# A conditional gated MLP with per-sequence adapters, recut from one fused pass over tiles into two phases with the activation spilled to DRAM

## The chip, the cores and the metric

The kernel runs on one core of one Trainium2 chip. The metric is device microseconds from start to end of one execution; lower is better. The engines named below are TensorE (PE in the profile, PEld for its weight loads), VectorE (DVE), ScalarE (ACT), GpSimd (POOL, which issues the indirect DMAs) and SyncE (SP, which issues the plain DMAs).

## What is computed

`x` is 64 sequences of 32 rows of 512 numbers. Each sequence has an adapter index (`itok_B_2_6`, 16 possible) for the rank-16 additions of the MLP, and a second index (`itok_B_0_15`) for a 32x32 mixing matrix over its rows. All is float32.

```python
def lora_add(base, inp, A, B):
    Ab = A[layer_idx][lora_indices]
    Bb = B[layer_idx][lora_indices]
    t = jnp.einsum('bri,bni->bnr', Ab, inp)
    return base + jnp.einsum('bor,bnr->bno', Bb, t) * SCALE
gate = lora_add(jnp.einsum('bnh,fh->bnf', x, W_gate), x, A_gate, B_gate)
up = lora_add(jnp.einsum('bnh,fh->bnf', x, W_up), x, A_up, B_up)
act = jax.nn.silu(gate) * up
down = lora_add(jnp.einsum('bnf,hf->bnh', act, W_down), act, A_down, B_down)
...
x = x + down                                  # F = 1376, H = 512, rank 16, SCALE 0.5
x = x + jnp.einsum('bct,bcd->bdt', x, weights[itok_B_0_15])   # 32x32 per sequence
```

## The kernel before

A tile is 4 sequences, 128 rows; there are 16 tiles, and one loop body (`tile`) does a whole tile on each engine. Every float32 product is made of three passes of a reduced-width type (fp32r): each operand is split into a high part (`hi`, a copy by ACT, L346) and a remainder (`lo`, a subtraction by DVE, L446), and PE multiplies hi*hi, hi*lo and lo*hi. The weights are loaded once through four slots of `landing`, split, and stay in SBUF for the whole run (`w_gate_hi`, `w_gate_lo`, `w_up_*`, `wd_*`).

In a tile PE computes gate and up in three sections of 352, 512 and 512 columns (`base`, L641 to L643, four blocks of 128 input features each), adds the adapters' part (`lora`, L650 and L651), transposes the gated activation through PE with an identity matrix (`turn_act`, L662, 11 chunks of 128 columns into the bank `ps_turn`), and multiplies the transposed chunks with the down weights (`down_chunks`, L673, 66 instructions of 288 columns). The down adapter (`down_lora`, L683) and the mixing (`mix`, L692) of a tile are done in the next tile, between its gate and up products, so that nothing waits for them. ACT does silu (L381) and the high parts, DVE the gating product (L528), the low parts, the masking and 32x32 turning of the adapters' small products (`mask_t`, `mask_td`), the two residual additions (`residual_h` L516, `residual_out` L523) and the spreading of the mixing matrix into a block diagonal `mix_w` (`spread_mix`, L509). POOL gathers by index: four of `a_raw` (the A factors of gate, up and down together), one of `b_raw` (all B factors, 3264 columns) and one of `mix_raw` (L322, L325, L333). SP loads `xT` and `x` and stores the result.

The order on every engine is written out by hand; engines meet only in semaphores. In `gathers(t)` POOL waits until the previous tile's `a_raw` and `b_raw` were split, gathers the next ones, and then waits for `mix_ready`, that is for `spread_mix` of the previous tile on DVE.

Of the kernel before, what the change touches and what calls it, by code (L numbers as in the profile page):

```python
# [17 lines left out]
TILES = SEQS // TILE_SEQS  # L42
KH = H // P
RR = TILE_SEQS * RANK
SECTIONS = [(0, F - 1024), (F - 1024, 512), (F - 512, 512)]
NS = len(SECTIONS)
SECTION_CHUNKS = [[(c, min(P, c0 + n - c)) for c in range(c0, c0 + n, P)] for c0, n in SECTIONS]
CHUNKS = [c for chunks in SECTION_CHUNKS for c in chunks]
FIRST_CHUNK = [sum(map(len, SECTION_CHUNKS[:s])) for s in range(NS + 1)]
SHORT = next(i for i, (_, n) in enumerate(CHUNKS) if n < P)  # L50
NC = len(CHUNKS)
TC = 2 * RR
A_GU = KH * 2 * RANK
A_ROW = A_GU + NC * RANK
B_ROW = 2 * F + H
WD = H + RR
HALF = WD // 2
HALVES = [slice(0, HALF), slice(HALF, H)]
PIECE = 1024
SLOTS = 4  # L60

def weight_pieces():

    pieces = [(m, s, k) for s in range(NS) for m in ("gate", "up") for k in range(0, KH, 2)]
    c = 0
    while c < NC:
        n = 1 if c == SHORT or c + 1 in (SHORT, NC) else 2
        pieces.append(("down", c, n))  # L70
        c += n
    return pieces

PIECES = weight_pieces()
GU_PIECES = sum(m != "down" for m, _, _ in PIECES)

def pieces_to(m, s, k):

    return PIECES.index((m, s, k - k % 2)) + 1

def pieces_to_chunk(c):
    return next(i for i, (m, at, n) in enumerate(PIECES) if m == "down" and at <= c < at + n) + 1

def build(nc, x, xT, w_gate, w_up, w_down, a_rows, b_rows, mix_rows, which, mult, lane, low, out):
    with ExitStack() as ctx:
        def sb(name, shape, dt=F32):  # L90
            return ctx.enter_context(nc.sbuf_tensor(name, shape, dt))

        def bank(name):
            return ctx.enter_context(nc.psum_tensor(name, [P, 512], F32))
# [3 lines left out]

        w_cols = {"gate": KH * (F + TC), "up": KH * F}
        w_hi = {m: sb(f"w_{m}_hi", [P, w_cols[m]], F32R) for m in ("gate", "up")}
        w_lo = {m: sb(f"w_{m}_lo", [P, w_cols[m]], F32R) for m in ("gate", "up")}
        wd_hi = sb("wd_hi", [P, NC, WD], F32R)
        wd_lo = sb("wd_lo", [P, NC, WD], F32R)
        landing = sb("landing", [P, SLOTS, PIECE])

        a_raw = sb("a_raw", [P, TILE_SEQS, A_ROW])
        b_raw = sb("b_raw", [P, B_ROW])
        b_gu = sb("b_gu", [P, 2 * F], F32R)  # L110
        b_dn = sb("b_dn", [P, H], F32R)

        xT_raw = sb("xT_raw", [P, KH * P])
        xT_hi = sb("xT_hi", [P, KH * P], F32R)
        xT_lo = sb("xT_lo", [P, KH * P], F32R)
        x_sb = sb("x_sb", [P, H])
        out_sb = sb("out_sb", [P, H])

        t_gu = sb("t_gu", [P, 2, 2 * RR])
        t_dn = sb("t_dn", [P, 2 * RR])  # L120
        tT_raw = sb("tT_raw", [P, 2, P])
        tdT_raw = sb("tdT_raw", [P, P])
        low_rows = sb("low_rows", [P, 1])
        tT_hi = sb("tT_hi", [P, 2, P], F32R)
        tT_lo = sb("tT_lo", [P, 2, P], F32R)
        tdT_hi = sb("tdT_hi", [P, P], F32R)
        tdT_lo = sb("tdT_lo", [P, P], F32R)
        act = [sb(f"act{i}", [P, 512]) for i in range(2)]
        actT_hi = sb("actT_hi", [P, NC, P], F32R)
        actT_lo = sb("actT_lo", [P, NC, P], F32R)  # L130

        mix_raw = sb("mix_raw", [P, CH])
        mix_w = sb("mix_w", [P, P])

        ident = sb("ident", [P, P])
        mask = sb("mask", [P, 2 * RR])
        which_sb = sb("which_sb", [P, TILES, TILE_SEQS + 2], I32)
        mult_sb = sb("mult_sb", [P, TILE_SEQS + 2], I32)
        lane_sb = sb("lane_sb", [P, TILE_SEQS + 2], I32)
        scaled = sb("scaled", [P, TILES, TILE_SEQS + 2], I32)  # L140
        rows = sb("rows", [P, TILES, TILE_SEQS + 2], I32)
        waited = sb("waited", [1, 1], I32)
        rows_now = sb("rows_now", [P, TILE_SEQS + 1], I32)
        mix_rows_now = sb("mix_rows_now", [P, 1], I32)

        ps_gate = [bank(f"ps_gate{i}") for i in range(2)]
        ps_up = [bank(f"ps_up{i}") for i in range(2)]
        ps_down = [bank(f"ps_down{i}") for i in range(2)]
        ps_turn = bank("ps_turn")
        ps_misc = bank("ps_misc")  # L150

        last_mix = [ps_misc, ps_up[1]]
# [4 lines left out]
        xT_landed = sem("xT_landed")  # L157
        x_landed = sem("x_landed")
        a_landed = sem("a_landed")
        b_landed = sem("b_landed")  # L160
        mix_landed = sem("mix_landed")
        stored = sem("stored")

        ident_zeroed = sem("ident_zeroed")
        ident_ready = sem("ident_ready")
# [4 lines left out]
        rows_copied = sem("rows_copied")  # L170
        mix_rows_copied = sem("mix_rows_copied")

        w_hi_ready = sem("w_hi_ready")
        xT_hi_ready = sem("xT_hi_ready")
        a_gu_hi_ready = sem("a_gu_hi_ready")
        b_gu_hi_ready = sem("b_gu_hi_ready")
        a_dn_hi_ready = sem("a_dn_hi_ready")
        b_dn_hi_ready = sem("b_dn_hi_ready")
        tT_hi_ready = sem("tT_hi_ready")
        low_rows_landed = sem("low_rows_landed")  # L180
        t_turned = sem("t_turned")
        td_turned = sem("td_turned")
        tdT_hi_ready = sem("tdT_hi_ready")
        silu_ready = sem("silu_ready")
        actT_hi_ready = sem("actT_hi_ready")

        w_ready = sem("w_ready")
        xT_ready = sem("xT_ready")
        a_gu_ready = sem("a_gu_ready")
        b_gu_ready = sem("b_gu_ready")  # L190
        a_dn_ready = sem("a_dn_ready")
        b_dn_ready = sem("b_dn_ready")
        t_gu_ready = sem("t_gu_ready")
        tT_ready = sem("tT_ready")
        t_dn_ready = sem("t_dn_ready")
        tdT_ready = sem("tdT_ready")
        act_ready = sem("act_ready")
        actT_ready = sem("actT_ready")
# [3 lines left out]

        t_done = sem("t_done")
        xT_used = sem("xT_used")
        section_done = sem("section_done")
        act_turned = sem("act_turned")
# [4 lines left out]
        def w_at(w, m, s, k, ks=1, with_a=False):  # L211

            c0, n = SECTIONS[s]
            extra = TC if m == "gate" else 0
            step = n + (extra if s == 0 else 0)
            at = KH * (c0 + (extra if s else 0)) + k * step
            part = w[:, at:at + ks * step].rearrange("p (k c) -> p k c", c=step)
            return part if with_a else part[:, :, 0:n]

        def a_part(w):

            n = SECTIONS[0][1]
            return w_at(w, "gate", 0, 0, KH, with_a=True)[:, :, n:n + TC].rearrange("p k (q c) -> p q k c", q=TILE_SEQS)

        t_ps = slice(SECTIONS[0][1], SECTIONS[0][1] + TC)

        def slot_view(n):

            m, at, k = PIECES[n]  # L230
            slot = landing[:, n % SLOTS, :]
            if m == "down":
# [20 lines left out]
        def _(sp):  # L253
# [15 lines left out]
            for n, (m, at, k) in enumerate(PIECES):  # L269
# [4 lines left out]
                if n >= SLOTS:  # L274
                    sp.wait_ge(w_ready, n - SLOTS + 1)
# [529 lines left out]
```

## Times and profile before

| | us |
|---|---|
| three runs | 507.98, 503.09, 508.24 (median 507.98) |
| the profiled execution: its own time | 507.72 |
| its span, first to last instruction | 505.9 |
| PE busy | 480.2 (95%) |
| DVE, ACT, POOL busy | 237.8, 159.4, 118.6 |
| mean granted TensorE clock | 0.983 |
| moved by DMA | 58.13 MB, 115 GB/s |

In rows of a group, "busy" is the sum of the durations, then the mean of one, then the engine's idle time just before them and what ended it. Matmuls overlap in the pipeline, so the mean duration of one is longer than the distance between two starts; the distance is what they cost. The chain of waits and work that ended last gives that distance directly.

### The profile page before, as it was taken

The page shows a single profiled execution, that of the slowest core. Times are in us where ns is not written, and L with a number is a line of the kernel's source. Part 1 is how long each engine was busy: PE and PEld are TensorE (multiplying, and loading weights), DVE is VectorE, ACT ScalarE, POOL GpSimd, SP SyncE. Part 2 cuts the span into 40 slices and gives each one's busy share as a digit, 9 for nine tenths or more (in the row PEclk, how much of TensorE's full clock was granted, in tenths as well). Part 3 has the DMA queues.
Part 4 walks back from the last instruction along what each step waited for, and adds up shares of the span by engine and source line. Part 5 has one row for each costly group of instructions (what it writes and reads, how often), then busy time and mean ns, then how long its engine had stood idle before and what let it go on. Part 6 is the DMA issues. An engine that isn't in the chain of part 4 may idle for free.

```text
span 505.9 us, 7251 instructions
## 1 busy us (share of the span) xinstructions
PE 480.2 (95%) x2716; PEld 430.2 (85%) x2716; DVE 237.8 (47%) x447; ACT 159.4 (32%) x244; POOL 118.6 (23%) x166
## 2 busy tenths in 40 slices
PE   2798599999999999999999999999999999999996
PEld 2677489899898989989898998989899898989985
DVE  2786525436353543635354362535536262553622
ACT  2764314232231424224142412414241241424120
POOL 5006040402305040220505022050502205050100
PEclk9799889999999999999999999999999999999998
DMA  7886151240604225060512406051240705123010
GB/s 246 325 263 228 60 200 48 64 180 1 223 21 171 73 74 171 1 223 21 171 73 78 167 1 224 19 183 62 87 157 2 230 12 195 50 92 132 1 41 21
DMA packets 16725, 58.13 MB, mean 115 GB/s; under 512 B 3184, under 2 KB 3696, under 8 KB 14672
## 3 DMA queue, kind: packets, MB, share of 16 engines
q0 software_dynamic: 5888, 36.97, 20.6%
q1 hardware_dynamic: 10832, 21.10, 12.9%
q8 instruction: 3, 0.05, 0.0%
q14 instruction: 2, 0.02, 0.0%
HBM read 53.86 MB, written 4.19 MB: 115 GB/s over the span
## 4 chain that ended last, share of the span: by engine, by line
PE 87%; DMA 4%; DVE 3%; POOL 3%; ACT 1%; issue 1%; SPq 0%; POOLq 0%; DVEq 0%
PE ps_down L673 26%; PE ps_gate L641 8%; PE ps_gate L643 8%; PE ps_gate L642 8%; PE ps_up L643 7%; PE ps_up L641 7%; PE ps_up L642 7%; PE ps_turn L662 4%; DMA b_raw<-in_b_rows,rows_now 3%; PE ps_misc L692 3%; POOL a_raw L322 3%; PE ps_gate L651 2%; PE ps_gate L650 2%; PE ps_up L650 2%; PE ps_up L651 2%; PE ps_down L683 2%
## 5 line engine op out<-in xcount | busy, mean ns | idle before, releaser
L446 DVE TENSOR_TENSOR actT_lo<-ps_turn,actT_hi 128x256 fp32r<-128x256 f32 (+1 forms) x64 | 32.0, 521 | 150.1 <-ACT actT_hi L346 115.4
L641 PE MATMUL ps_gate<-w_gate_hi,xT_hi 128*128 128x512 f32 (+3 forms) x196 | 77.8, 397 | 12.8 <-DVE w_gate_lo L446 12.8
L346 ACT ACTIVATE actT_hi<-ps_turn 128x256 fp32r<-128x256 f32 (+1 forms) x64 | 27.9, 461 | 165.6 <-PE ps_turn L662 162.1
L643 PE MATMUL ps_gate<-w_gate_hi,xT_lo 128*128 128x512 f32 (+3 forms) x196 | 77.3, 394 | 0.0
L642 PE MATMUL ps_gate<-w_gate_lo,xT_hi 128*128 128x512 f32 (+3 forms) x196 | 76.8, 392 | 0.0
L673 PE MATMUL ps_down<-wd_hi,actT_hi 128*128 128x288 f32 (+1 forms) x352 | 76.6, 299 | 0.0
L673 PE MATMUL ps_down<-wd_hi,actT_lo 128*128 128x288 f32 (+1 forms) x352 | 75.5, 295 | 0.0
L673 PE MATMUL ps_down<-wd_lo,actT_hi 128*128 128x288 f32 (+1 forms) x352 | 75.5, 296 | 0.0
L641 PE MATMUL ps_up<-w_up_hi,xT_hi 128*128 128x512 f32 (+1 forms) x192 | 74.1, 386 | 0.4 <-DVE w_up_lo L446 0.4
L331 POOL COPY mix_rows_now<-rows 128x1 int32 (+1 forms) x16 | 3.0, 187 | 300.4 <-DVE mix_w L509 300.4
L643 PE MATMUL ps_up<-w_up_hi,xT_lo 128*128 128x512 f32 (+1 forms) x192 | 71.3, 371 | 0.0
L322 POOL DMA_INDIRECT a_raw<-in_a_rows,rows_now x64 | 66.5, 1039 | 19.8 <-issue 19.8
L642 PE MATMUL ps_up<-w_up_lo,xT_hi 128*128 128x512 f32 (+1 forms) x192 | 70.9, 369 | 0.0
L469 DVE SCALAR_TENSOR_TENSOR b_gu<-b_raw,low_rows,b_gu 128x2752 fp32r<-128x2752 f32 x16 | 49.4, 3085 | 29.2 <-ACT b_gu L346 29.2
L673 PEld LDWEIGHTS ps_down<-wd_hi,actT_hi 128*128 128x128 f32 (+1 forms) x352 | 57.3, 189 | 1.6 <-issue 0.2
L673 PEld LDWEIGHTS ps_down<-wd_hi,actT_lo 128*128 128x128 f32 (+1 forms) x352 | 56.8, 188 | 0.0
L673 PEld LDWEIGHTS ps_down<-wd_lo,actT_hi 128*128 128x128 f32 (+1 forms) x352 | 56.7, 188 | 0.0
L641 PEld LDWEIGHTS ps_gate<-w_gate_hi,xT_hi 128*128 128x128 f32 x196 | 38.5, 196 | 19.3 <-issue 8.7
L528 DVE TENSOR_TENSOR act<-act,ps_up 128x512 f32<-128x512 f32 (+1 forms) x48 | 30.2, 630 | 31.1 <-issue 26.9
L643 PEld LDWEIGHTS ps_gate<-w_gate_hi,xT_lo 128*128 128x128 f32 x196 | 38.2, 195 | 7.3
L642 PEld LDWEIGHTS ps_gate<-w_gate_lo,xT_hi 128*128 128x128 f32 x196 | 38.5, 196 | 6.2
L381 ACT ACTIVATE act<-ps_gate 128x512 f32<-128x512 f32 (+1 forms) x48 | 26.4, 550 | 50.7 <-PE ps_up L651 45.7
(66 smaller groups left out, 628.7 us busy)
## 6 DMA issues: line engine op xcount, KB each, us to landing
xT_raw<-in_xT SPq DMA_DIRECT2D x16, 256.0 KB, 2.6
x_sb<-in_x SPq DMA_DIRECT2D x16, 256.0 KB
out<-out_sb SPq DMA_DIRECT2D x15, 256.0 KB
landing<-in_w_down SPq DMA_DIRECT2D x5, 512.0 KB, 4.7
landing<-in_w_gate SPq DMA_DIRECT2D x4, 512.0 KB, 5.2
landing<-in_w_up SPq DMA_DIRECT2D x4, 512.0 KB, 4.8
a_raw<-in_a_rows,rows_now POOLq DMA_INDIRECT x64
landing<-in_w_gate SPq DMA_DIRECT2D x2, 352.0 KB, 3.8
```

What stands on the lines that cost most here:

```text
L322: pool.indirect_dma_start(a_raw[:, q, :], None, a_rows, bass.IndirectOffsetOnAxis(ap=rows_now[:, q:q + 1], axis=0)).then_inc(a_landed, 16)
L346: return nc.scalar.activation(dst, src, ACT.Copy)
L381: nc.scalar.activation(act[s % 2][:, 0:n], ps_gate[s % 2][:, 0:n], ACT.Silu).then_inc(silu_ready, 1)
L446: return nc.vector.tensor_tensor(dst, src, hi_part.bitcast(F32), ALU.subtract)
L469: return nc.vector.scalar_tensor_tensor(b, raw, low_rows[:, :], b.bitcast(F32), ALU.mult, ALU.subtract)
L528: nc.vector.tensor_tensor(act[s % 2][:, 0:n], act[s % 2][:, 0:n], ps_up[s % 2][:, 0:n], ALU.mult)\
L641: pe.matmul(ps[:, cols], x_hi, hi, start=(k == 0 and not columns), stop=False)
L642: pe.matmul(ps[:, cols], x_hi, lo, start=False, stop=False)
L643: last = pe.matmul(ps[:, cols], x_lo, hi, start=False, stop=stops and k == KH - 1)
L650: pe.matmul(ps[:, 0:n], tT_hi[:, g, :], b, start=False, stop=False, skip_group_check=True)
L651: return pe.matmul(ps[:, 0:n], tT_lo[:, g, :], b, start=False, stop=True, skip_group_check=True)
L673: last = pe.matmul(ps_down[half][:, 0:HALF], a[0:k, c, :], w[0:k, c, half * HALF:(half + 1) * HALF], start=(c == 0 and a is actT_hi and w ...
```

## The change

There are now two phases. Phase 1 takes tiles by pairs (8 pairs): its six units are the three sections for the one and the other tile, with three pairs of gate and up banks in turn and the adapters' part of a unit one unit late. The tiles of a pair take every second sequence, so that a 32x32 block transpose on DVE (`gating`, now followed by a transpose into `staging`) gives blocks that SP writes to a DRAM tensor `actT_dram` in runs of 64 numbers (256 bytes), four DMAs for a section of a pair (`spill`). The PE transposes, the identity and `ps_turn` are gone. The B factors come by section, six gathers for a pair instead of one for a tile; the weights come in pieces of one 128-row block.

Phase 2 takes the 16 tiles one by one: SP loads the transposed activation (`load_actT`, 704 KB), ACT and DVE split it, PE does `down_chunks` 0 to 2, the down adapter of the tile before, chunks 3 to 6, the mixing of the tile before, and chunks 7 to 10. The A and B factors of down and the mixing matrix are gathered for each tile in this phase (`gather_down`). The A factors have one raw buffer and go to either side of the down weights in turn (`wd_a`).

```diff
+            def gather_down(m, first=False):
+                at = TILE_SEQS + 1
+                reached(pool, a_dn_ready, m)
+                pool.tensor_copy(a_dn_now[:, :], now(m)[:, at:at + TILE_SEQS]).then_inc(a_dn_now_copied, 1)
+                indirect_after(a_dn_now_copied, m + 1)
+                for q in range(TILE_SEQS):
+                    gather(a_dn_raw[:, q, :], a_dn_rows, a_dn_now[:, q:q + 1]).then_inc(a_dn_landed, 16)
+                reached(pool, mix_ready, m)
+                pool.tensor_copy(mix_now[:, :], now(m)[:, at + TILE_SEQS + 1:COLS]).then_inc(mix_now_copied, 1)
+                indirect_after(mix_now_copied, m + 1)
+                gather(mix_raw[:, :], mix_rows, mix_now[:, :]).then_inc(mix_landed, 16)
+                reached(pool, b_dn_ready, m)
...
+                indirect_after(b_dn_now_copied, m + 1)
+                gather(b_dn_raw[:, :], b_dn_rows, b_dn_now[:, :]).then_inc(b_dn_landed, 16)
...
+            def spill(pr, s):
+                c0, n = SECTIONS[s]
+                sp.wait_ge(act_turned, NU * pr + 2 * s + 2)
+                for q in range(TILE_SEQS):
+                    at = (q % 2) * 2 * BLOCK
+                    sp.dma_start(
+                        actT_dram[bass.ds(2 * pr + q // 2, 1), c0:c0 + n, at:at + 2 * BLOCK]
+                        .rearrange("o (j f) c -> f (o j) c", f=BLOCK),
+                        staging[s][q * BLOCK:(q + 1) * BLOCK, :, :, :].rearrange("f j t c -> f j (t c)"))\
+                        .then_inc(spilled[s], 16)
...
+                reached(ve, spilled[s], 64 * pr)
+                ve.wait_ge(act_ready, NU * pr + k + 1)
+                nc.vector.transpose(staging[s][:, :, t, :], act[k % 2][:, 0:n].rearrange("p (j c) -> p j c", c=BLOCK))\
+                    .then_inc(act_turned, 1)
...
+            def pair(pr, final=False):
+                base(pr, 0)
+                lora(pr - 1, 5)
+                for k in range(1, NU):
+                    base(pr, k, final=final and k == NU - 1)
+                    lora(pr, k - 1)
...
+            def split_a_dn(m, e):
+                sc.wait_ge(a_dn_landed, 16 * TILE_SEQS * (m + 1))
+                reached(sc, down_done, m - 1)
+                hi(wd_a(wd_hi, e), a_dn_raw.rearrange("p q (c r) -> p q c r", c=NC)).then_inc(a_dn_hi_ready, 1)
...
+            def down(m, e, first=False, last=False):
+
+                if not first:
+                    mask_td(m - 1, 1 - e)
+                    spread_mix(m - 1)
+                if not last:
+                    split_a_dn(m + 1, 1 - e)
+                if not first:
+                    residual_h(m - 1, 1 - e)
+                if not last:
+                    split_actT(m + 1, 1 - e)
+                split_b_dn(m)
+                if not first:
+                    residual_out(m - 1, 1 - e)
...
+            def down(m, e, first=False):
+                pe.wait_ge(a_dn_ready, m + 1)
+                pe.wait_ge(actT_ready, m + 1)
+                reached(pe, h_ready, 2 * (m - 1))
+                down_chunks(m, e, 0, 3)
                 if not first:
+                    down_lora(m - 1, 1 - e)
+                down_chunks(m, e, 3, 7)
                 if not first:
+                    reached(pe, out_ready, m - 1)
+                    mix(m - 1, 1 - e, [ps_mix, ps_mix])
+                down_chunks(m, e, 7, NC).then_inc(down_done, 1)
```

The first `down` is DVE's, the second PE's; both run once for each tile of phase 2. The places where the change moves instructions are on POOL and on DVE. POOL's loop of before (one turn for each tile) reads, with the wait in brackets:

```order
L318 ISA [waits b_dn_ready,a_dn_ready]
L318 COPY rows_now<-rows 128x5
L309 TENSOR_TENSOR waited<-lane_sb 1x1 [waits rows_copied]
L322 DMA a_raw<-in_a_rows,rows_now 128x304 x4
L325 DMA b_raw<-in_b_rows,rows_now 128x3264
L331 ISA [waits mix_ready]
L331 COPY mix_rows_now<-rows 128x1
L309 TENSOR_TENSOR waited<-lane_sb 1x1 [waits mix_rows_copied]
L333 DMA mix_raw<-in_mix_rows,mix_rows_now 128x32
```

POOL's loop of phase 2 of the changed kernel, again one turn for each tile, reads:

```order
L402 ISA [waits a_dn_ready]
L402 COPY a_dn_now<-rows 128x4
L362 TENSOR_TENSOR waited<-lane_sb 1x1 [waits a_dn_now_copied]
L368 DMA landing<-in_a_dn_rows,a_dn_now 128x176 x4
L407 ISA [waits mix_ready]
L407 COPY mix_now<-rows 128x1
L362 TENSOR_TENSOR waited<-lane_sb 1x1 [waits mix_now_copied]
L368 DMA mix_raw<-in_mix_rows,mix_now 128x32
L411 ISA [waits b_dn_ready]
L411 COPY b_dn_now<-rows 128x1
L362 TENSOR_TENSOR waited<-lane_sb 1x1 [waits b_dn_now_copied]
L368 DMA b_dn_raw<-in_b_dn_rows,b_dn_now 128x512
```

The B gather has moved behind the wait for `mix_ready`, and has a copy and a helper instruction of its own; the four A gathers of the next turn stand behind both.

On DVE, the loop of before had this piece between the down product of one tile and the residual of the same tile:

```order
L509 COPY mix_w<-mix_raw 32x32 [waits mix_landed]
L509 COPY mix_w<-mix_raw 32x32 x3
L515 ISA [waits x_landed]
L516 TENSOR_TENSOR x_sb<-x_sb,ps_down 128x288 [waits down_lora_done]
L515 REGISTER_ALU
L516 TENSOR_TENSOR x_sb<-x_sb,ps_down 128x224 [waits down_lora_done]
L446 TENSOR_TENSOR wd_lo<-a_raw,wd_hi 128x4x11x16 [waits a_dn_hi_ready]
L469 SCALAR_TENSOR_TENSOR b_dn<-b_raw,low_rows,b_dn 128x512 [waits b_dn_hi_ready]
```

DVE's turn for an even tile in phase 2 of the changed kernel reads, at the same place (`landing` is here the raw buffer of the A factors for `wd_lo`, and of the transposed activation for `actT_lo`):

```order
L766 COPY mix_w<-mix_raw 32x32 [waits mix_landed]
L766 COPY mix_w<-mix_raw 32x32 x3
L736 REGISTER_ALU
L589 TENSOR_TENSOR wd_lo<-landing,wd_hi 128x4x11x16 [waits a_dn_hi_ready]
L770 REGISTER_ALU
L772 REGISTER_ALU [waits x_landed0]
L773 TENSOR_TENSOR x_sb<-x_sb,bank 128x224 [waits down_lora_done]
L772 REGISTER_ALU
L773 TENSOR_TENSOR x_sb<-x_sb,bank 128x288 [waits down_lora_done]
L589 TENSOR_TENSOR actT_lo<-landing,actT_hi 128x1280 [waits actT_hi_ready]
```

The low part of the A factors, `wd_lo`, stood behind the residual `x_sb` and now stands ahead of it. It is the part for the tile after the one that PE is working on, while the residual is for the tile before it.

## Rows read from the trace of the kernel before

**Rows 1.** The page: busy time, share of the span, instructions.
```profile
PE 480.2 (95%) x2716; PEld 430.2 (85%) x2716; DVE 237.8 (47%) x447; ACT 159.4 (32%) x244; POOL 118.6 (23%) x166
```
**Rows 2.** Chain that ended last, one steady tile: start us, us, what.
```profile
88.05 0.22 PE ps_gate L641
...
92.59 0.48 PE ps_down L683 x4
...
96.49 0.86 PE ps_misc L692 x4
...
100.12 0.33 PE ps_turn L662 x3
...
106.83 0.44 PE ps_turn L662 x4
...
108.22 2.40 PE ps_down L673 x18
110.62 0.44 PE ps_turn L662 x4
111.06 6.39 PE ps_down L673 x48
117.45 0.22 PE ps_gate L641
```
**Rows 3.** Timeline of the last tile's end: start us, us, engine, line, what, [idle before].
```profile
499.43 0.29 DVE L479 TENSOR_TENSOR t_dn<-ps_down,mask 128x128 f32<-128x128 f32 x1 [5.07 <-PE ps_down L673]
500.65 0.72 DVE L509 COPY mix_w<-mix_raw 32x32 f32<-32x32 f32 x4
501.43 0.75 DVE L516 TENSOR_TENSOR x_sb<-x_sb,ps_down 128x288 f32<-128x288 f32 x2
502.03 0.72 PE L692 MATMUL ps_misc<-x_sb,mix_w 128*128 128x288 f32 x2 [0.49 <-DVE x_sb L516]
```
**Rows 4.** Timelines of DVE (first row) and POOL around one steady tile's gathers.
```profile
239.42 0.73 DVE L509 COPY mix_w<-mix_raw 32x32 f32<-32x32 f32 x4
...
240.32 0.19 POOL L331 COPY mix_rows_now<-rows 128x1 int32 x1 [20.29 <-DVE mix_w L509]
...
242.63 0.19 POOL L318 COPY rows_now<-rows 128x5 int32 x1
...
243.41 0.99 POOL L322 DMA_INDIRECT a_raw<-in_a_rows,rows_now  x1 [0.33 <-issue]
...
247.22 0.95 POOL L322 DMA_INDIRECT a_raw<-in_a_rows,rows_now  x1 [0.30 <-issue]
```
**Rows 5.** DMA issues: what, queue, count, KB each, us from issue to landing.
```profile
lane_sb<-in_lane SPq DMA_DIRECT2D x1, 3.0 KB, 2.1
```
**Rows 6.** Groups of instructions: the splits of the down A factors.
```profile
L346 ACT ACTIVATE wd_hi<-a_raw 128x704 fp32r<-128x704 f32 x16 | 12.4, 777 | 0.0
...
L446 DVE TENSOR_TENSOR wd_lo<-a_raw,wd_hi 128x704 fp32r<-128x704 f32 x16 | 14.2, 884 | 0.0
```
**Rows 7.** Stretches: bounds us, length, busy of PE, PEld, DVE, ACT, POOL, clock, DMA share, GB/s.
```profile
211.70:214.20 2.50, 2.50 (x14) 2.14 (x13) 1.32 (x2) 0.13 (x1) 2.06 (x4) 1.00 0.02 7
...
60.40:66.00 5.60, 5.56 (x15) 4.59 (x16) 3.24 (x9) 1.57 (x3) 3.27 (x6) 0.52 0.03 6
...
85.00:445.00 360.00, 360.00 (x2075) 324.89 (x2075) 167.90 (x320) 106.43 (x172) 85.00 (x120) 1.00 0.30 103
```
**Rows 8.** Timeline of PE and of gathers in the start; columns as in rows 3.
```profile
8.33 0.63 PE L641 MATMUL ps_gate<-w_gate_hi,xT_hi 128*128 128x352 f32 x1 [8.33 <-DVE w_gate_lo L446]
9.31 0.95 POOL L322 DMA_INDIRECT a_raw<-in_a_rows,rows_now  x1 [0.30 <-issue]
14.68 0.63 ACT L346 ACTIVATE w_gate_hi<-a_raw 128x512 fp32r<-128x512 f32 x1 [6.53 <-DMA a_raw<-in_a_rows,rows_now]
...
60.44 0.61 PE L683 MATMUL ps_down<-b_dn,tdT_hi 128*128 128x288 f32 x1 [5.72 <-DVE tdT_lo L446]
```
**Rows 9.** DMA queues: packets, MB, time of their packets as a share of 16 engines.
```profile
q1 hardware_dynamic: 10832, 21.10, 12.9%
```

More of the change, by code:

```diff
@@ L51 @@
+NU = len(UNITS)
+TC = 2 * RR
+S0 = SECTIONS[0][1]
+W0 = TC + S0 + TC
+CHUNKS = [(c, min(P, F - c)) for c in range(0, F, P)]
 NC = len(CHUNKS)
-TC = 2 * RR
+LAST = CHUNKS[-1][1]
 A_GU = KH * 2 * RANK
[L54 to L72, printed above, removed]
@@ L75 @@
-PIECES = weight_pieces()
-GU_PIECES = sum(m != "down" for m, _, _ in PIECES)
-def pieces_to(m, s, k):
[L81 to L88, printed above, removed]
+A_DN = NC * RANK
+WD = RR + H + RR
+HALF = (RR + H) // 2
+PIECE = 512
+SLOTS = 5
+SETS = 3
+COLS = 2 * TILE_SEQS + 3
+PIECES = [(m, s, k) for s in range(NS) for m in ("gate", "up") for k in range(KH)]
@@ L209, in build, with reached, w_block @@
         mix_done = sem("mix_done")
-        def w_at(w, m, s, k, ks=1, with_a=False):
+        def reached(engine, semaphore, value):
+            if not isinstance(value, int) or value > 0:
+                engine.wait_ge(semaphore, value)
+        def w_block(w, m, s):
             c0, n = SECTIONS[s]
[L215 to L219, printed above, removed]
@@ new lines, in _ @@
+            pair(0, first=True, weights=[(GU_PIECES, GU_PIECES + SLOTS)])
+            pair(1, weights=[(GU_PIECES + SLOTS, GU_PIECES + SLOTS + 3), (GU_PIECES + SLOTS + 3, len(PIECES))])
+            with sp.Fori(2, PAIRS - 1) as pr:
+                pair(pr)
+            pair(PAIRS - 1, last=True)
+            sp.wait_ge(w_ready, len(PIECES))
+            load_actT(0, 0)
+            spill(PAIRS - 1, 2)
+            sp.wait_ge(xT_used[0], PAIRS)
+            sp.wait_ge(xT_used[1], PAIRS)
+            load_x(0, 0)
@@ L338, in _, with indirect_after, now, gather @@
-            gathers(0, first=True)
-            with pool.Fori(1, TILES) as t:
-                gathers(t)
+            def indirect_after(semaphore, value, cell=0):
+                pool.wait_ge(semaphore, value)
+                pool.tensor_tensor(waited[:, cell:cell + 1], lane_sb[0:1, 0:1], lane_sb[0:1, 0:1], ALU.add)
+            def now(tile):
+                return rows[:, bass.ds(tile, 1), :].rearrange("p o c -> p (o c)")
+            def gather(dst, src, offsets):
+                return pool.indirect_dma_start(dst, None, src, bass.IndirectOffsetOnAxis(ap=offsets, axis=0))
@@ new lines, in spread_mix, with residual_h @@
+            def spread_mix(m):
+                ve.wait_ge(mix_landed, 16 * (m + 1))
+                for q in range(TILE_SEQS):
+                    r = slice(q * CH, (q + 1) * CH)
+                    last = nc.vector.tensor_copy(mix_w[r, r], mix_raw[r, :])
+                last.then_inc(mix_ready, 1)
+            def residual_h(m, e):
+                ve.wait_ge(x_landed[e], 16 * (m // 2 + 1) if isinstance(m, int) else 8 * (m + 2 - e))
+                for half, (cols, at) in enumerate(down_halves(e)):
+                    ve.wait_ge(down_lora_done, 2 * m + half + 1)
+                    nc.vector.tensor_tensor(x_sb[e][:, cols], x_sb[e][:, cols],
+                                            ps_down[e][half][:, at:at + cols.stop - cols.start],
+                                            ALU.add).then_inc(h_ready, 1)
@@ L732, in _, with mix @@
-            pe.wait_ge(ident_ready, 1)
-            tile(0, first=True)
-            with pe.Fori(1, TILES) as t:
-                tile(t)
-            down_lora(TILES - 1)
-            mix(TILES - 1, last_mix)
+            def mix(m, e, outs):
+                pe.wait_ge(mix_ready, m + 1)
+                for half, (cols, _) in enumerate(down_halves(e)):
+                    pe.wait_ge(h_ready, 2 * m + half + 1)
+                    at = cols if outs[0] is outs[1] else slice(0, cols.stop - cols.start)
+                    pe.matmul(outs[half][:, at], mix_w[:, :], x_sb[e][:, cols], start=True, stop=True)\
+                      .then_inc(mix_done, 1)
```

1079 lines of the change are left out of this document (619 added, 460 removed).

## Prediction

> **What bounds the kernel now.** I read the busy times first: PE is busy 95% of the span, the next engine 47% [rows 1]. Then the chain that ended last, where it is steady: from the start of one tile's gate product to the next is 117.45 - 88.05 = 29.40 us, and every piece of it is PE [rows 2]. So a tile costs what PE's instructions cost, one after the other, and 16 x 29.4 = 470 us of the 505.9 are that. The reader should also see who is not late: POOL sits idle 20.29 us in each tile before it gathers [rows 4]. That wait costs nothing in this kernel, because some 20 us of other PE work lie between the gathers and their use. The whole question is whether this cover is still there after the change.
>
> **What PE saves.** In the steady tile the transposes through PE take 0.33 + 0.44 + 0.44 = 1.21 us [rows 2], 19.4 us over 16 tiles. The down product is 2.40 + 6.39 = 8.79 us, the down adapter 0.48, the mixing 0.86 [rows 2]. What is left, 29.40 - 1.21 - 8.79 - 0.48 - 0.86 = 18.06 us, is gate, up and their adapters. Phase 1 therefore has 36.1 us of PE work for a pair, phase 2 has 8.79 + 0.48 + 0.86 = 10.13 us for a tile. If both phases kept PE full, the kernel would win. In phase 1 nothing else comes near 36 us: the gathers are 14 for a pair at 1.25 us from one start to the next ((247.22 - 243.41)/3 [rows 4]), 17.5 us. I cost phase 1 at PE's pace.
>
> **What phase 2 must wait for.** A turn now has only 10.13 us of PE work for POOL to hide its gathers behind, so I follow the semaphores round one turn. Call D the moment when PE ends a tile's down product; say tile m-1. DVE's turn m begins with the masking of that product and the spreading of the mixing matrix, then needs the low part of the A factors of tile m+1, and only then does the residual of tile m-1. PE wants this residual for the mixing in the middle of tile m, and cannot end tile m before it. POOL may not gather the mixing matrix of tile m until the spreading is done, and the A factors of tile m+1 stand behind that gather and the one of B in its queue. That is a closed ring, with one turn for each tile:
>
> - D to the end of the four spreading copies: 500.65 + 0.72 - 499.43 = 1.94 us [rows 3], which holds the masking, the turn, ACT's high part and the copies.
> - DVE to POOL: 240.32 - (239.42 + 0.73) = 0.17 [rows 4].
> - POOL, mixing gather with its copy and helper: 242.63 - 240.32 = 2.31 [rows 4].
> - POOL, B gather with the new copy and helper: 0.78 from copy to gather (243.41 - 242.63), 0.95 for a gather and 0.03 to the next: 1.76 [rows 4].
> - POOL, copy to the start of the fourth A gather: 247.22 - 242.63 = 4.59 [rows 4].
> - That gather's start to its landing. No row shows a small gather landing with the queues free. A load of 3 KB takes 2.1 us from issue to landing [rows 5]; the first tile's last A gather took 14.68 - 9.31 = 5.37 us while the weights came in [rows 8]. These are the ends. 90 KB on quiet queues are nearest to the small load, plus half a microsecond since POOL's descriptors take 0.95 us to write: I take 2.6.
> - ACT's high part 0.78, DVE's low part 0.88 [rows 6], 0.1 between them: 1.76.
> - The residual's first half until the mixing starts: 502.03 - 501.43 = 0.60 [rows 3].
>
> Sum: 15.7 us after D. PE has had 18 down instructions, the adapter and 24 more by then: 42 x 0.133 (6.39/48 [rows 2]) + 0.48 = 6.1 us. So it stands idle for 9.6 us in every turn. What follows on it is the mixing, 0.86, and the last 24 down instructions, 24 x 0.133 = 3.20: 4.06 us, if the clock holds. The trace says that it does not: after a wait of 5.72 us [rows 8] PE ran from 60.4 to 66.0 at a granted clock of 0.52 [rows 7], the lower of its two levels (1.2 GHz), and so I let the first 5.3 us after the wait do half the work, 2.65 us' worth, and the rest, 1.41, run full: 6.7 us. A turn is 15.7 + 6.7 = **22.4 us** against 10.13 us of work. Bounds: clock never falling 15.7 + 4.06 = 19.8; all of it at half 15.7 + 8.1 = 23.8; landing at its ends -0.5 or +2.8.
>
> For the fixed part of a gather the Trainium skill (DMA: Bandwidth & Descriptors, Anatomy of one DMA, SWDGE path) gives about 2.0 us plus bytes over 436 GB/s. By that page the landing would be an estimated 2.2 us, the turn 22.0, and the total some 6 us less than mine; the sum here goes by the rows.
>
> The other traffic of phase 2 does not decide. The activation's load is issued at the end of a turn and is wanted about 15 us later. The b split and `residual_out` follow the residual on DVE and are done before the next D.
>
> **The rest of the sum.**
> - Pair 0. PE starts at 8.33 [rows 8]; full speed would end the pair at 8.3 + 36.1 + about 2 for a low clock = 46. Eight A gathers now stand ahead of the first B gather: the fourth started at 9.31 before [rows 8], the eighth starts near 15.1 and lands 5.4 later, near 21. The second set of eight stands ahead of section 1's B factors, and the weight pieces' splits are queued behind both on ACT. I add 11 us of waits: 57. Bounds 46, and 65, a few us above the 60.4 at which PE came out of its last long wait of the start before [rows 8].
> - Pairs 1 to 7: 7 x 36.1 = 253, to 310.
> - Handover. The last adapter product, then ACT's silu, the splits of A and of 1408 activation columns on ACT and DVE: down(0) starts at about 315 and ends at about 325; the second activation load is issued only after the last spill, and DVE is free for the ring at about 328.5.
> - Fourteen turns of the ring (the last A factors are those of tile 15): 14 x 22.4 = 314, to 642.
> - Tile 15 without the ring 10.1, to 652; then the end as now: from t_dn at 499.43 [rows 3] to 505.9 is 6.5, to 658.8.
>
> The profiled run of before took 507.72 with a span of 505.9, 1.8 more; so 658.8 + 1.8 = **661 us**. The median before is 507.98, the profiled run is at its level.
>
> **Spills, where only bounds are to be had.** The spill writes 5504 packets of 256 bytes for a pair (44,032 in all). The mean packet of the plain queue took 0.129 x 16 x 505.9 us / 10832 = 96 ns [rows 9]; at that price a pair's spill holds 16 engines for 33 us. The mixing gather, 128 rows of 128 bytes, shows a share of 0.02 in 2.5 us [rows 7], 0.8 us of engine time or 6 ns a row: 2 us a pair. The steady share of before, 0.30 [rows 7], makes 18 us for two tiles, of which about 3 are x and the result, now in phase 2: 15 stay. So 17 to 48 us for a pair of 36. I take nothing, since the mean packet is 2 KB and these are an eighth of it.
>
> **Rivals.**
> 1. The forecast, ring of 20 to 26 us and PE-bound phase 1: 0.76, time 661; its own range, from its bounds, 620 to 700.
> 2. Phase 1 bound by the spill: small writes at the price of the mean packet, 48 us a pair. Adds 12 x 8 = 96: 757. For it speaks the number of packets, against it their size and the margin of 19 us a pair. 0.12. The Trainium skill (DMA: Bandwidth & Descriptors, Specifications) says that transfers under 512 bytes are read, modified and written back and miss line rate; by that rule this rival gains, but no row of before has small writes to DRAM.
> 3. The clock stays up in phase 2, since PE works 10 us of each 20: 14 x 2.6 less, 625. One row speaks against. 0.08.
> 4. Not slower than before: the ring does not close, because the A factors land before they are wanted, and phase 2 runs at PE's pace. Then 315 + 8.8 + 15 x 10.13 + 6.5 + 1.8 = 484. It needs a turn of under about 11 us: with 328.5 + 14 turns + 18.4 the level of 508 is at 11.5. POOL alone takes 0.17 + 2.31 + 1.76 + 4.59 + 0.95 = 9.8 us a turn and starts 1.9 us after D. 0.04.
>
> **Numbers.** The likeliest case gives 661. The range takes in its own bounds and rival 3, and part of rival 2 (a spill that costs a few us a pair): 618 to 710. One per cent is about what a measurement of this kernel can tell from no change. Faster by over 1%: 0.03; within 1%: 0.01; slower by over 1%: 0.96.
>
> **What the changed profile would show.** Right: phase 1 with PE full and a pair every 36 us until about 310; then a PE that is busy half the time, a wait of 8 to 11 us before each mixing, named for DVE (`x_sb`); DVE waiting for ACT's `wd_hi`, ACT for the A gather's landing, POOL for DVE's `mix_w`; the clock low in phase 2; turns of 22 us. Wrong: waits of SP or DVE on the spills and pairs of well over 36 us (rival 2); turns near 20 with the clock near 1 (rival 3); PE full in phase 2 (rival 4). A landing of the small gather far from 2.6 us would move the total 14 us for each microsecond.

## The result, and the profile after

The changed kernel takes 642.9 us (641.91 to 643.96) against 508.11 us: the ratio is 1.268, with a 95% interval of 1.259 to 1.277. The forecast was 661 us in a range of 618 to 710. The span of the profiled execution is 640.2 us. Every ratio here and below is to runs of the kernel before taken beside it (medians 506.9 to 508.1).
The page of the changed kernel: busy times, granted clock in 40 slices, and PE's share in them.

```profile
PE 493.6 (77%) x2552; PEld 435.3 (68%) x2552; DVE 271.1 (42%) x512; ACT 162.8 (25%) x261; POOL 250.4 (39%) x404
...
PE   4789999999999999999685476447744675447647
...
PEclk9999999999999999999987987688767977798779
...
PE 56%; POOL 15%; issue 10%; DMA 9%; DVE 6%; ACT 3%; SPq 1%; POOLq 0%; DVEq 0%
```

Against [rows 1] PE is still the busiest engine, but the first half of the span is full and the second is not, and the clock falls in the second half alone. The last line is the chain that ended last: POOL and DMA, which had no part in a steady tile before [rows 2], now hold a quarter of it.

Two stretches of the changed kernel, one in phase 1 and one over 13 turns of phase 2 (bounds, length, busy of PE, PEld, DVE, ACT, POOL, clock, DMA share, GB/s; in [rows 7] the steady kernel of before):

```profile
118.00:154.00 36.00, 36.00 (x168) 30.32 (x167) 19.12 (x30) 11.49 (x18) 16.53 (x26) 1.00 0.53 147
336.00:609.00 273.00, 162.84 (x994) 154.95 (x993) 76.85 (x182) 38.73 (x65) 92.92 (x163) 0.80 0.31 89
```

Phase 1 keeps PE full at full clock. In phase 2 PE is busy 60% of the time at a mean clock of 0.80, while no other engine is busy even 35% of it: nothing there is short of capacity. Who waits for whom, longest first:

```profile
POOL mix_now L407 <- DVE mix_w L766: 180.4, 15, 13.0
ACT wd_hi L437 <- DMA landing<-in_a_dn_rows,a_dn_now: 167.7, 15, 12.1
DVE wd_lo L589 <- ACT wd_hi L437: 163.9, 15, 11.9
PE bank L934 <- DVE x_sb L773: 119.2, 15, 9.2
```

These four are one ring read backwards, 15 times each: POOL waits for the spread mixing matrix, ACT for the A factors that POOL gathered, DVE for ACT's high part, PE for the residual that stands behind it on DVE. The wait of POOL was there before too, and longer (20.29 us [rows 4], now 12.0 in the mean), and cost nothing.

The chain of the changed kernel through one turn, from the end of one tile's down product, where DVE begins to mask it (459.27), to the landing of the next A factors (start us, us, what):

```profile
459.27 0.30 DVE t_dn L753
...
461.04 0.19 DVE mix_w L766
...
461.39 0.19 POOL mix_now L407
...
462.11 0.98 POOL mix_raw L368
463.09 0.20 POOL b_dn_now L411
...
464.71 0.20 POOL a_dn_now L402
...
465.32 0.99 POOL landing L368
...
469.11 2.56 DMA landing<-in_a_dn_rows,a_dn_now
```

The splits and the residual follow (2.09 us), and the turn ends so:

```profile
473.76 2.07 PE bank L934 x4
475.83 4.09 PE bank L914 x24
```

Every link that the prediction named is there, in its order. The turn is 20.65 us: 1.95 + 0.17 + 1.70 + 1.62 + 4.40 + 2.56 + 2.09 + 2.07 + 4.09. The mean over the 13 turns between the first mixing product (348.18) and the fourteenth (617.63) is 20.73 us.

### The profile page after: what moved, and what is told of

It is laid out like the page before. It is cut to its first block, busy times and chain, and to the rows that moved or that the text cites. A ratio compares the mean times of both kernels' runs of the same rounds, so it can differ in the third digit from the quotient of the medians.

```text
span 640.2 us, 7780 instructions
## 1 busy us (share of the span) xinstructions
PE 493.6 (77%) x2552; PEld 435.3 (68%) x2552; DVE 271.1 (42%) x512; ACT 162.8 (25%) x261; POOL 250.4 (39%) x404
## 4 chain that ended last, share of the span: by engine, by line
PE 56%; POOL 15%; issue 10%; DMA 9%; DVE 6%; ACT 3%; SPq 1%; POOLq 0%; DVEq 0%
PE bank L835 12%; PE bank L836 12%; PE bank L837 12%; PE bank L914 10%; POOL landing L368 6%; DMA landing<-in_a_dn_rows,a_dn_now 6%; PE bank L934 5%; PE bank L880 3%; PE bank L879 3%; POOL a_raw L368 3%; POOL mix_raw L368 2%; ACT wd_hi L437 2%; DVE mix_w L766 1%; DMA b_raw<-in_b_rows,b_now 1%; POOL waited L362 1%
## 5 line engine op out<-in xcount | busy, mean ns | idle before, releaser
L914 PE MATMUL bank<-wd_hi,actT_hi 128*128 128x288 f32 (+1 forms) x352 | 87.4, 332 | 7.8 <-DVE actT_lo L589 7.8
L835 PE MATMUL bank<-w_gate_hi,xT_hi 128*128 128x512 f32 (+3 forms) x200 | 77.5, 388 | 9.1 <-DVE w_gate_lo L589 8.1
L914 PE MATMUL bank<-wd_lo,actT_hi 128*128 128x288 f32 (+1 forms) x352 | 80.9, 313 | 0.0
L914 PE MATMUL bank<-wd_hi,actT_lo 128*128 128x288 f32 (+1 forms) x352 | 80.1, 311 | 0.0
L835 PE MATMUL bank<-w_up_hi,xT_hi 128*128 128x512 f32 (+1 forms) x192 | 72.4, 377 | 6.2 <-DVE w_up_lo L589 5.6
L836 PE MATMUL bank<-w_gate_lo,xT_hi 128*128 128x512 f32 (+3 forms) x200 | 77.0, 385 | 0.0
L837 PE MATMUL bank<-w_gate_hi,xT_lo 128*128 128x512 f32 (+3 forms) x200 | 77.0, 385 | 0.0
L914 PEld LDWEIGHTS bank<-wd_hi,actT_hi 128*128 128x128 f32 (+1 forms) x352 | 65.8, 214 | 11.1 <-issue 8.4
L836 PE MATMUL bank<-w_up_lo,xT_hi 128*128 128x512 f32 (+1 forms) x192 | 72.2, 376 | 0.0
L837 PE MATMUL bank<-w_up_hi,xT_lo 128*128 128x512 f32 (+1 forms) x192 | 72.2, 376 | 0.0
L368 POOL DMA_INDIRECT landing<-in_a_dn_rows,a_dn_now x64 | 62.0, 969 | 17.5 <-issue 17.5
```

What stands on the lines that cost most here:

```text
L368: return pool.indirect_dma_start(dst, None, src, bass.IndirectOffsetOnAxis(ap=offsets, axis=0))
L835: pe.matmul(out_, x_hi, hi, start=(first and k == 0), stop=False)
L836: pe.matmul(out_, x_hi, lo, start=False, stop=False)
L837: last = pe.matmul(out_, x_lo, hi, start=False, stop=(stops and k == KH - 1))
L914: last = pe.matmul(ps_down[e][half][:, 0:HALF], a[e][0:n, c, :], w[0:n, c, at:at + HALF], start=(c == 0 and a is actT_hi and w is wd_hi), ...
```

## The experiments

The first six start from the changed kernel, the others each add to an earlier one. "Turn" is the distance between two mixing products on PE in phase 2, the mean over 13 turns unless said otherwise.

### Cut the ring on POOL

```diff
-            with pool.Fori(1, TILES) as m:
-                gather_down(m)
...
+            with pool.Fori(1, TILES - 1) as m:
+                gather_a_dn(m + 1)
+                gather_mix(m)
+                gather_b_dn(m)
...
```

`gather_down` is cut into its three parts here; it had the A factors of tile m, its mixing matrix and its B factors in this order.

> Changed kernel (642.9 us) with one edit on GpSimd in phase 2: the four gathers of the A factors of tile m+1 are issued ahead of the mixing and B gathers of tile m, so that they no longer stand behind the wait for mix_ready. Same instructions, same bytes. Theory (closed ring through GpSimd's queue): the A factors now land before they are wanted, the turn of 20.7 us falls to TensorE's work of 10.1 to 10.5 us, 14 turns give back about 147 us: 492 to 503 us, granted clock near 1. Rival (phase 2 is bound by how much GpSimd and the DMA engines have to do for a tile, not by the order): no change, 638 to 648 us.

Measured: 530.35 us, ratio to the kernel before 1.045 (1.041 to 1.049). One change of order gives back 112.6 of the 134.8 us, with the same instructions and bytes, so the order was the cause and not the amount of work. But the turn is 12.69 us, not 10.1 to 10.5: the time is 27 us above the upper end of the expectation. The chain shows what took the place of the ring, one turn of it:

```profile
404.80 1.95 POOL landing L368
...
408.63 0.95 POOL landing L368
...
409.89 5.36 DMA landing<-in_a_dn_rows,a_dn_now
415.27 0.80 ACT wd_hi L449
416.09 0.90 DVE wd_lo L601
...
417.95 1.95 POOL landing L368
```

There is one raw buffer for the A factors, so the next gathers wait until `wd_lo` has read it: gather, land, split, gather. The landing now takes 5.4 us where it took 2.56, and the first gather 1.95 us where it took 0.99. The trace puts both beside other work: SyncE issued the activation's load 0.9 us ahead of that landing (409.00), and the first gather overlaps DVE's `actT_lo` by 1.28 us.

### Cut the ring on DVE

```diff
                 if not first:
+                    residual_h(m - 1, 1 - e)
+                if not last:
                     split_a_dn(m + 1, 1 - e)
-                if not first:
-                    residual_h(m - 1, 1 - e)
```

> Changed kernel with one edit on VectorE in phase 2: residual_h of tile m-1 ahead of the low part of the A factors of tile m+1, GpSimd's order as it was. Theory: the mixing no longer waits, but the product of tile m+1 still starts only when A factors and activation are split, 1.95 + 0.17 + 1.70 + 1.62 + 4.40 + 2.53 + about 4.0 = 16.4 us after the end of tile m-1, so two turns take 16.4 + 10.1 = 26.5 us, 13.3 us each (to 14.5 with a low clock): 540 to 560 us. Rival (work of GpSimd and DMA binds): no change. Rival (the ring needs only to be cut once, anywhere): as the first experiment, about 497 us.

Measured: 601.81 us, ratio 1.189 (1.184 to 1.193), turn 17.63 us. The mixing no longer waits; PE's wait has moved to the first down product of a tile (`actT_lo`, 80.9 us in 16 waits). The turn lost 3.1 us and not the 7.4 of the theory. All three stated outcomes are missed, each by over 40 us. The chain of this run:

```profile
433.83 2.56 DMA landing<-in_a_dn_rows,a_dn_now
...
437.11 1.46 ACT actT_hi L437 x2
...
440.29 0.66 DVE b_dn L593
440.95 0.60 DVE out_sb L783
441.55 0.21 DVE t_dn L753
...
443.57 0.19 POOL mix_now L407
```

My expectation let a new turn of the ring begin when PE ends a product. But DVE is in order: the masking `t_dn` of the finished product stands behind `actT_lo`, `b_dn` and `out_sb` of the same turn, which wait for the A factors' landing through ACT. The ring is closed a second time, by DVE's queue instead of PE's, 451.30 - 433.83 = 17.5 us round.

### Take one gather out of the ring

```diff
-            with pool.Fori(1, TILES) as m:
-                gather_down(m)
...
+            with pool.Fori(1, TILES - 1) as m:
+                gather_mix(m)
+                gather_a_dn(m + 1)
+                gather_b_dn(m)
...
```

> Changed kernel with one edit on GpSimd in phase 2: the order in a turn is mixing gather of tile m, A gathers of tile m+1, B gather of tile m, so only the B gather (1.62 us from copy to the next copy in the trace) leaves the ring. Theory: each of 14 turns is 1.6 us shorter, 620 us (616 to 624). Rival (order does not matter): no change.

Measured: 630.16 us, 12.7 less than the changed kernel, where 22.9 were expected, and above the expected range. The turn is 19.59 us, 1.14 shorter. The trace shows the link 1.60 us shorter, as it should be (the first A gather starts 1.60 us behind the mixing gather, 458.89 against 457.29, instead of 444.44 against 441.24, 3.20), but from the start of the mixing to the end of the product 6.54 us pass in the mean over 13 turns where 6.14 did. That gives back 0.4 of the 1.6 us, and it is the clock: behind PE's wait the granted clock is 0.50 for 4.7 us in the mean of these turns, where it was for 3.9 us, and half of that difference is 0.4. The total follows: 13 x 1.14 = 14.8 less, but the first mixing product comes 1.1 us later (349.29 against 348.18) and the last turn is 0.6 longer (12.38 against 11.80), together 13.1.

### Both cuts

> Both edits of the first two experiments together. Theory: TensorE binds with the first edit alone, so the second adds nothing: within 3 us of the first experiment, 490 to 503 us. If a rest of the ring is left in the first experiment (a turn well over 10.1 us), this one is faster than it by that rest.

Measured: 523.92 us, ratio 1.032 (1.028 to 1.037), 6.4 us less than the first cut alone. The turn is 12.07 us in the mean, 10.1 to 14.0. The first clause of the expectation fails with that of the first cut, by over 20 us; the second holds: there was a rest, and a part of it is gone.

### Keep PE busy while it waits

```diff
                 down_chunks(m, e, 3, 7)
                 if not first:
+                    for _ in range(60):
+                        pe.matmul(banks[2][:, 0:HALF], actT_hi[e][:, 0, :], wd_hi[:, 0, RR * e:RR * e + HALF],
+                                  start=True, stop=True)
```

> Changed kernel with 60 more products of 288 columns in each turn of phase 2, into a bank that nobody reads, at the place where TensorE waits 8.5 us for the residual. 60 x 0.133 = 8.0 us, so they end before the wait does. Theory (the turn ends with the mixing and 24 products at half the clock): the clock stays at 1, the mixing takes 0.86 instead of 2.07 us and the 24 products 3.2 instead of 4.0, a turn is 2.0 us shorter with more work in it: 642.9 - 14 x 2.0 = 615 us (611 to 620). Rival (the low clock in phase 2 is a symptom that costs nothing, GpSimd's side sets the turn): no change, 638 to 648 us.

Measured: 628.61 us, ratio 1.240 (1.235 to 1.245): 14.3 us less than the changed kernel with 900 more products. Over 260 us of phase 2:

```profile
340.00:600.00 260.00, 251.03 (x1846) 246.14 (x1845) 79.81 (x187) 41.45 (x69) 96.51 (x166) 1.00 0.33 96
```

and the end of a turn:

```profile
447.26 1.13 PE bank L934 x4
448.39 3.18 PE bank L914 x24
```

The clock is 1.00 where it was 0.80, the mixing and the 24 products take 4.31 us where they took 6.16, and the turn is 18.95 us, 1.8 shorter. That the low clock costs 1.8 us a turn is shown. The expectation had 2.0, since it set the mixing at 0.86 us. That is its distance where other products run right ahead of it (629.59 in the changed kernel's chain); here PE had stood 0.64 us, and at full clock the mixing takes 1.13. The total lies above the expected range of 611 to 620 mainly since the added 8 us hide only where there is a wait: in the first and the last turn there is none, and the first mixing product comes 3.9 us later (352.06 against 348.18) and the last turn is 6.3 us longer (18.12 against 11.80). 13 x 1.8 - 3.9 - 6.3 = 13, against 12.2 between the spans of the two profiled executions.

### Spill twice

```diff
+                    sp.dma_start(
+                        actT_dram2[bass.ds(2 * pr + q // 2, 1), c0:c0 + n, at:at + 2 * BLOCK]
+                        .rearrange("o (j f) c -> f (o j) c", f=BLOCK),
+                        staging[s][q * BLOCK:(q + 1) * BLOCK, :, :, :].rearrange("f j t c -> f j (t c)"))\
+                        .then_inc(spilled[s], 16)
```

> Changed kernel with every spill DMA issued twice, the second time into another DRAM tensor, waits counted to match. Theory (the spill hides behind phase 1): a pair stays at 36.4 us, the total grows by less than 4 us, up to 647 us, all of it at the handover; DMA share in phase 1 rises from 0.53 by about 0.1. Rival (small writes cost like the mean packet, 96 ns, or SyncE's issues hold up the rest): a pair would need 15 + 2 x 33 = 81 us of the DMA engines, phase 1 grows by over 100 us.

Measured: 650.52 us, 7.6 more than the changed kernel, where less than 4 were expected. The same stretch of phase 1 as above:

```profile
118.00:154.00 36.00, 35.46 (x164) 29.34 (x163) 21.30 (x33) 12.40 (x20) 17.41 (x28) 1.00 0.76 190
```

The DMA share goes from 0.53 to 0.76, over twice the rise that was expected: 0.23 x 36 x 16 = 132 us of engine time for 5504 packets, 24 ns for one of 256 bytes. Over five pairs (68.65 to 250.61 us there, 70.01 to 252.97 here) it goes from 0.56 to 0.74, which makes 19 ns. Both are at most a quarter of the 96 ns that were the upper bound [rows 9]. A pair takes 36.6 us instead of 36.4. Between the two profiled executions (spans 649.5 and 640.2) 3.3 us are lost by the end of phase 1 and 6.0 more by the first mixing product, where the wait before the first down product grows from 5.5 to 9.2 us and the last spill, now eight DMAs, holds up the second activation load. So the rival is ruled out: one spill is hidden in phase 1, and twice as much nearly so, but at the handover it is not.

### Two raw buffers for the A factors

```diff
-        a_dn_now = sb("a_dn_now", [P, TILE_SEQS], I32)
+        a_dn_now = [sb(f"a_dn_now{t}", [P, TILE_SEQS], I32) for t in range(2)]
+        a_dn_raw = [landing[:, NC * P:NC * P + TILE_SEQS * A_DN].rearrange("p (q c) -> p q c", q=TILE_SEQS),
+                    sb("a_dn_raw1", [P, TILE_SEQS, A_DN])]
...
+            def gather_a_dn(m, e):
+                reached(pool, a_dn_ready, m - 1)
...
+                gather_mix(2 * j)
+                gather_b_dn(2 * j)
+                gather_a_dn(2 * j + 2, 0)
...
```

> Both edits of the third run, and a second raw buffer (with its own index buffer and semaphore) for the A factors of odd tiles, so that the gathers of tile m+2 need not wait until those of m+1 are split. In the third run a turn still took 12.3 us against 10.13 of TensorE. Theory (what is left is a second, smaller ring: gathers, landing, split, buffer free, gathers): a turn falls to 10.2 to 11.0 us, 523.9 - 14 x 1.7 = 500 us (495 to 506). Rival (what is left is contention of gathers and loads on the DMA engines, landings of 5 us where they took 2.5): the turn stays over 12 us, 520 to 526 us.

Measured: 509.36 us, ratio 1.005 (1.002 to 1.008), 14.6 us less than with one buffer. The "third run" is *Both cuts*. The turn is 10.88 us, as the theory has it, and the total 3.4 us above its range. The landings of the A factors on its chain still take 5.1 to 5.2 us, so what the rival named is there and no longer binds. The second, smaller ring was real; the buffer and the gathers that it lets POOL issue a tile earlier came together and were not tried apart.

### The handover

```diff
+                if last:
+                    sp.wait_ge(w_ready, len(PIECES))
+                    load_actT(0, 0)
                 for s in range(2):
...
-            load_actT(0, 0)
-            spill(PAIRS - 1, 2)
...
+            load_actT(1, 1)
             load_x(0, 0)
-            load_actT(1, 1)
+            spill(PAIRS - 1, 2)
...
             split_actT(0, 0)
+            silu(PAIRS - 1, 4)
             silu(PAIRS - 1, 5)
...
```

> The run before this one, and at the change from phase 1 to phase 2: SyncE issues the first activation load ahead of the last spills and the second ahead of the very last one; ScalarE and VectorE split the first activation ahead of the silu and gating of units 4 and 5. Theory: down(0) starts right behind the last adapter product, 5 us earlier, and down(1) no longer waits for its load, some 4 us more: 9 us less than the run before, 491 us (485 to 498), under the 508 of the kernel before. Rival (the handover is hidden by the first turns' gathers): 0 to 3 us less.

Measured: 501.48 us, ratio 0.990 (0.986 to 0.994), 7.9 us less than the run before it; the first down product starts at 316.2 us instead of 324.4. The gain is as expected in kind and within 1.1 us in size, the total 3.5 us above the expected range. The turn stays at 10.98 us. The chain of this run names the next wait:

```profile
415.76 0.36 SPq L315
416.45 0.38 SPq L300
417.03 4.13 DMA landing<-actT_dram
421.45 1.47 ACT actT_hi L461 x2
```

L315 is the store of a result, L300 and the DMA behind it the load of the next activation: SyncE's queue had put the load behind the store's wait for `residual_out`.

### The load ahead of the store

```diff
-                store(2 * j - 1, 1)
                 load_actT(2 * j + 2, 0)
+                store(2 * j - 1, 1)
                 load_x(2 * j + 1, 1)
...
```

> The run before (two buffers, handover), with SyncE's order in phase 2 changed: the load of the activation of tile m+2 ahead of the store of tile m-1, so that it no longer waits for residual_out and is issued a turn earlier. Turns were 10.1 to 11.8 us there, 10.9 in the mean, with ScalarE waiting for that load. Theory: turns fall to 10.1 to 10.4 us, 14 x 0.6 = 8 us less than 501.5: 493 us (489 to 497). Rival (the landings of the A gathers, 5 us where they took 2.5, hold the turn up; the load would only collide elsewhere): 499 to 504 us.

Measured: 493.51 us, ratio to the kernel before 0.974 (0.969 to 0.979). The turn is 10.34 us; time and turn are in the ranges expected. 150 us of phase 2 read:

```profile
336.00:486.00 150.00, 146.48 (x1051) 142.26 (x1049) 89.43 (x208) 41.56 (x69) 102.26 (x158) 1.00 0.57 164
```

PE is busy 98% of it at full clock. This is the version that beats both kernels: the two-phase cut is 2.6% faster than the fused one when its second phase is ordered so that PE binds.

### B ahead of A in the first pair

```diff
+                if first:
+                    gather_b(pr, 1, 0)
+                    gather_b(pr, 1, 1)
                 if not last:
                     gather_a(pr + 1, 0)
                     gather_a(pr + 1, 1)
-                for s in range(1, NS):
+                for s in range(2 if first else 1, NS):
```

> The run before this one, and in pair 0 the two B gathers of section 1 ahead of the eight A gathers of pair 1 on GpSimd. TensorE waits some 9 us in pair 0 from 25 to 52 us, and the chain there went through those eight gathers, the B landing, its split and the weight splits queued behind it. Theory: the waits after 40 us go, 3 to 5 us less than the run before. Rival (the weights' own landing and splitting set the pace): within 1 us of it.

Measured: 496.87 us (494.0 to 500.6), ratio 0.982 (0.978 to 0.987). The gain of 3 to 5 us is not there; the median is 3.4 us above that without the edit, with runs that overlap. In the two profiled executions PE's waits for the low parts of weights go from 9.1 + 5.6 to 7.6 + 11.6 us, and the first adapter product of pair 1 comes 4.3 us later (73.47 against 69.20). The longest of these waits is now 7.9:

```profile
PE bank L863 <- DVE w_up_lo L617: 11.6, 3, 7.9
```

and the chain ahead of it names why:

```profile
43.35 4.49 DMA b_raw<-in_b_rows,b_now
47.87 1.06 ACT b_gu L464
48.96 1.28 DVE b_gu L621
50.24 0.61 DVE w_up_lo L617
50.90 0.79 PE bank L863
```

The edit did what it was meant to: the gate weights of section 2 are split on ACT at 34.92 instead of 40.14. But the B gathers of section 1, now first, wait for their buffer until 23.4 and 27.4 us, so the eight A gathers behind them start at 30.1 instead of 21.0, and the B gather of section 2 behind those goes out at 43.35 instead of 39.50. Its split stands ahead of the up weights' splits on ACT, which come at 48.83 instead of 44.24. The wait was moved by one section, and grew.

## Why the prediction was right

**What bounds it, and PE's saving.** Right. Phase 1 runs at PE's work: 36.39 us for a pair ((250.61 - 68.65)/5 between the adapter products of the same unit), forecast 36.1. The reordered kernel that keeps PE full in phase 2 takes 493.5 us, a ratio of 0.974, 13.8 us less than the kernel before as measured beside it (507.29). Of the 19.4 us of transposes that the cut removes, most comes through once nothing waits: a tile costs 36.47/2 + 10.34 = 28.6 us there against 29.40 [rows 2], 13 us for 16 tiles. That the 13 us are the transposes is argued from these distances; no run puts them back.

**The ring.** Right, with its place and direction, and shown by the cuts: one reordering on POOL takes 8.0 us from a turn, one gather moved out of it 1.1, the low clock 1.8. Its sum was 1.75 us too long for the turn above, 20.65 instead of 22.4:

| link | forecast | measured |
|---|---|---|
| end of down to mixing matrix spread | 1.94 | 1.95 |
| DVE to POOL | 0.17 | 0.17 |
| mixing gather | 2.31 | 1.70 |
| B gather | 1.76 | 1.62 |
| to the fourth A gather | 4.59 | 4.40 |
| landing | 2.6 | 2.56 |
| splits and residual to the mixing | 2.36 | 2.09 |
| mixing and 24 products | 6.7 | 6.16 |

The largest miss is the mixing gather. In [rows 4] it took 1.56 us of issue itself (2.31 from copy to copy), here 0.98. The price was taken from a stretch in which DVE ran `wd_lo` and the B factors' split beside it, and now DVE is idle. The other is the end: the low clock was set at 5.3 us from [rows 7], and over 13 turns the granted clock was 0.50 for 3.9 us in the mean (3.0 to 6.1) from the start of the mixing. The sum also had 0.86 us for the mixing at full clock, the distance of a mixing in a running stream; behind a wait it takes 1.13 us at full clock (*Keep PE busy while it waits*) and 2.07 at the low one, 1.8 times as long. The two misses of this term go opposite ways, which is luck.

**The landing.** The one link that no row showed was forecast at 2.6 us between ends of 2.1 and 5.4, and took 2.47 to 2.65 in 14 of 14 turns. That it fits so closely is in part luck: the half microsecond added to the small load's 2.1 came from no row. The Trainium skill's figure (DMA: Bandwidth & Descriptors, Anatomy of one DMA, SWDGE path) would have been an estimated 2.2, some 0.3 us too short here. The landing was also not a constant: beside a 640 KB load it took 3.2 to 6.0 us on the chains of the reordered kernels, up to and above the upper end.

**The rest of the sum.** Pair 0 and the seven pairs: PE's last adapter product of phase 1 ends at 314.5, forecast 310, 4.5 late; 1.7 of that are seven pairs at 36.39 instead of 36.1 and 253, the rest is pair 0. The first turn of the ring begins at 333.7 instead of 328.5, 5.2 late, so the handover adds 0.7 us of its own; the second activation load, behind the last spill as foreseen, took 5.06 us to land (324.73 in the chain). Turns: 14 x 1.67 less. Tile 15 and the end: 10.1 and 6.5, as forecast. 658.8 + 5.2 - 23.4 = 640.6, against a span of 640.2. So the total is nearer than the turns alone: the late start makes up for a part of their excess, which is luck too.

**The spill.** The chosen 0 was right; its price lies at 19 to 24 ns between the bounds of 6 and 96. The Trainium skill says that transfers of under 512 bytes miss line rate (DMA: Bandwidth & Descriptors, Specifications). The trace agrees in direction: with 256 bytes in 19 to 24 ns an engine moves 11 to 13 GB/s, against 1.95 KB in 96 ns, 20 GB/s, for the mean packet of before [rows 9]. It did not bind.

**The rivals.** Rival 2 and rival 4 did not happen. Rival 3 (the clock stays up) did not either: 0.80 over phase 2. Its price, 2.6 us a turn, was 1.8 by the run that kept the clock up.

**What I would have missed.** The prediction did not need the second rings, since the first hid them. The experiments' expectations did, and failed on them twice: on the single raw buffer (27 us above the range) and on DVE's in-order queue (42 us above it).

## What to carry to other kernels

A wait that costs nothing is paid for by the work beside it; when a change takes a loop's work from 29 to 10 us, list every wait of the loop that was longer than the new loop, and follow each round the queues until it closes. A ring goes through in-order queues as well as through semaphores, and behind the ring that binds stands the next one: cut it, look at the chain again, and expect only the difference to the next. Where in its queue a gather or a load is issued, with one more buffer, was worth 149 us here (642.9 to 493.5), against some 13 for what PE no longer computes.

## What the runs showed of the hardware

- After a wait of 8.5 us in each turn PE ran its next 3.0 to 6.1 us at a granted clock of 0.50, and a stretch of extra products in the wait kept it at 1.00: 900 more products made the kernel 14 us faster.
- The four products of a mixing took 0.86 us in a running stream, 1.13 behind a pause of 0.64 us at full clock, and 2.07 behind a wait at the low clock.
- An indirect gather's issue takes 0.95 to 0.99 us on POOL when DVE is idle, and as long beside most of DVE's work. In most turns of the first cut and of both cuts it takes 1.8 to 2.3 us where it overlaps the 1280-column subtraction `actT_lo` (404.80 and 417.95 us in the trace of the first cut). But a gather at 332.76 us there overlaps it for 0.86 us and takes 0.95. That DVE is the cause was seen from the overlap alone and not tested.
- The landing of the same 90 KB gather took 2.5 to 2.7 us on quiet queues and 3.2 to 6.0 us where a load of 640 KB in 512-byte runs was issued within 3 us of the gather. The load as the cause was seen from this alone and not tested.
